# A later wait for the group-mean matrix, row loads issued one per key store, and unread products on TensorE around the attention

## The chip, the cores and the metric

One core of a Trainium2 chip runs the whole program in one launch. The metric is the device time of one execution in microseconds. The core has TensorE (PE, with its weight loads shown as PEld), VectorE (DVE), ScalarE (ACT), GpSimd (POOL) and SyncE (SP), which run side by side and wait for each other on semaphores. SyncE, ScalarE and GpSimd each issue DMA transfers on a queue of their own (q1, q10 and q0 in the profile), and 16 DMA engines serve all queues.

## The reference

The input x is four images of 128 channels and 96 x 96 pixels. Two layers follow each other:

```
x = x + L0(_gn(x))        # group norm over 32 groups of 4 channels, then attention over channels
x = x + L1(_gn(x))        # group norm, then sign, 3x3 conv, batch norm, sign, 3x3 conv, batch norm, + identity

L0: kv = dw3x3(einsum(qkv_w, x));  k, v = split(kv)
    q  = idwt2(dw3x3 of the four bands of dwt2(x))       # wavelet transform, convs, inverse transform
    q, k normalised along the pixels;  attn = softmax(q k^T * temperature) in each of 8 heads of 16 channels
    out = proj_w @ (attn @ v)
L1: out = conv3x3(sign(x), sign(w1)*alpha1);  out = sign(batchnorm(out))
    out = batchnorm(conv3x3(out, sign(w2)*alpha2)) + x
```

## The kernel before

The program has four blocks. Each is a set of five instruction streams, one for each engine, and a block begins when all streams of the one before it have ended.

**Block 1, `block_stats_and_projections`** (lines 187 to 530). For every image it takes the statistics for the group norm and multiplies the image with the key and value weights. An image has 24 chunks of 4 rows (384 pixels); 4 chunks are a piece, so there are 6 pieces an image and 24 in all, counted n = 0 to 23. For each piece TensorE makes 4 key chunks and 4 value chunks, ScalarE copies them out of PSUM (line 477), VectorE makes the low half of the keys (line 429), and two stores of 784 KB leave: the keys from SyncE's queue (line 288), the values from ScalarE's queue (line 481). Both go through a ring of three buffers: before ScalarE writes the first key chunk of piece n it waits until the key store of piece n - 3 has landed. After the store of piece 6, SyncE also issues seven constants for block 2 (lines 296 to 298), and then eight loads of x rows (`load_x_rows`, line 175), each 144 KB in runs of 384 bytes, for the first two channel groups. The store of piece 7 comes behind them in SyncE's stream. These loads write into the memory of image 0, which is why they wait until image 0 is used up.

**Block 2, `block_grams`**. It makes queries, keys and their gram matrices, channel group by channel group. It is bound by TensorE for 670 us and is not changed, but for products added behind its last instruction on TensorE, `gram_null` (line 1121).

**Block 3, `block_attention`** (lines 1201 to 1376). It works on matrices of 16 x 16 numbers. TensorE and VectorE take turns: products `rows` (lines 1358, 1359) and 32 small ones (1365); VectorE lines 1285 to 1304; product `pn` (1369); VectorE and ScalarE to line 1320; product `pq` (1372); `abd` (1331); four products (1375); the copy of `pa_t` (1337) ends the block. Meanwhile SyncE loads the weights of the convolutions, and then image 0 of x and of the values in halves (lines 1258, 1259, 2304 KB each, signals `s_v0` and `s_x0`).

**Block 4, `block_convolutions`** (lines 1379 to 1770). For each image, TensorE projects the values (`project`, line 1749), VectorE adds x (`add_x`, line 1631) and takes statistics (1635), `group_mean` multiplies them with the matrix `gmean` (1738), ScalarE takes the signs (1537), and TensorE convolves (1761) while it projects the next image. x lives in `xs`, which has room for two images. GpSimd loads images 1 to 3 into it (`load_x`, line 1503) and stores the finished sums of images 0 and 1 (line 1513), each in four parts, and waits for each part to land before it issues the next: load of image 1, store of image 0, load of image 2, store of image 1, load of image 3. VectorE waits for all four parts of image b + 1 before its first `add_x` of that image.

The matrix `gmean` (64 KB) is loaded by SyncE at the start of block 4 with signal `s_c`. TensorE and VectorE both wait for `s_c` before their first instruction of the block, though only `group_mean` reads the matrix, and it first runs after the 24 projections of image 0.

Of the kernel before, what the change touches and what calls it, by code (L numbers as in the profile page):

```python
# [22 lines left out]
F32 = mybir.dt.float32  # L23
F16 = mybir.dt.float16
# [160 lines left out]
def block_stats_and_projections(nc, d, p):  # L185

    with ExitStack() as ctx:
# [83 lines left out]
        def _(sp):  # L271
# [13 lines left out]
            for n in range(NIMG * NPC):  # L285
# [4 lines left out]
                if n == NPC:  # L290
# [7 lines left out]
                    sp.dma_start(early["null_cols"], d["null_cols"].partition_broadcast(W)).then_inc(p["s_c"], 16)  # L298
                    for i in range(2):
                        for im in range(NIMG):  # L300
                            load_x_rows(sp, d, early, im, i, i, p["s_xin"][i])
                if n == (NIMG - 1) * NPC:
# [227 lines left out]
def block_grams(nc, d, p):  # L530
# [5 lines left out]
    with ExitStack() as ctx:  # L536
# [518 lines left out]
        def _(pe):  # L1055
# [140 lines left out]
            for e in range(GPARTS - 1):  # L1196
                gram_part(HEADS - 1, (HEADS - 1) % 2, e, 0, len(units[e]), last_banks[e], e > 0)
            gram_null(HEADS - 1, last_banks[GPARTS - 1], True)


def block_attention(nc, d, p):

    with ExitStack() as ctx:
# [28 lines left out]
        pn = ctx.enter_context(nc.psum_tensor("b3_pn", [C, 512], F32))  # L1232
        pp = ctx.enter_context(nc.psum_tensor("b3_pp", [C, 512], F32))

        s_in, s_g, s_gst = p["s_in"], p["s_g"], p["s_gst"]
# [114 lines left out]
        def _(pe):  # L1350
            pe.wait_ge(s_in, NSMALL * 16)
            pe.wait_ge(s_g, 32)
            pe.wait_ge(s_gst, GRAMS_IN)

            def rows(bank, sel, one, two, last, stop=True):

# [7 lines left out]
            for n in range(HI):  # L1364
                ins = nc.tensor.matmul(ps[0:HD, n * HD:(n + 1) * HD], gram[:, n, 2, :], pick[:, HD:2 * HD],
                                       start=False, stop=(n == HI - 1))
            ins.then_inc(s_p, 1)
            pe.wait_ge(s_go, 1)
            nc.tensor.matmul(pn[0:HD, 0:HI * HD], ones[:], krow[:].rearrange("p n e -> p (n e)"),
                             start=True, stop=True).then_inc(s_p, 1)  # L1370
            pe.wait_ge(s_go, 2)
            nc.tensor.matmul(pq[:, 0:HI * HD], copies[:], att[:].rearrange("p n e -> p (n e)"), start=True, stop=True).then_inc(s_p, 1)
# [6 lines left out]
def block_convolutions(nc, d, p):  # L1379
# [5 lines left out]
    with ExitStack() as ctx:  # L1385
# [222 lines left out]
        def _(dve):  # L1608
# [66 lines left out]
            dve.sem_inc(s_y, NBK)  # L1675
            dve.wait_ge(s_c, 16)
            for half in range(2):
# [54 lines left out]
        def _(pe):  # L1732
            pe.wait_ge(s_c, 16)

            def group_mean(b):
# [31 lines left out]
            for half in range(2):  # L1767
                pe.wait_ge(p["s_v0"][half], 16)
                with pe.Fori(half * RND // 2, (half + 1) * RND // 2) as r:
                    for k in range(RC):  # L1770
                        project(0, r, k)
            group_mean(0)
            for b in range(NIMG - 1):
# [110 lines left out]
```

## Time and profile before

| | |
|---|---|
| median of 3 runs | 1374.42 us (1373.09 to 1375.93) |
| profiled execution | 1371.92 us, of which the span of instructions 1370.0 us |
| PE busy | 1182.8 us (86%) |
| DVE busy | 1025.6 us (75%) |
| ACT busy | 889.5 us (65%) |
| POOL busy | 433.7 us (32%) |
| blocks, from the timeline | block 1: 0 to 187 us; block 2: to 879; block 3: to 906; block 4: to 1370 |

A timeline row gives the start, the duration, the engine, the line, the operation and its tiles, the count of instructions merged in it, and in brackets how long the engine was idle before it and what released it. `SPq` and `POOLq` are the sequencers. The table of windows gives for each stretch the busy time and count of instructions of every engine, then the granted clock of TensorE (1.00 is 2.4 GHz, 0.50 is 1.2 GHz), the share of the 16 DMA engines' time that was in use, and GB/s.

### The profile page before, as it was taken

Reading aid. Unit: us, or ns where it says so; the run is one execution under the profiler, and the core shown is the slowest. Engines: PE = TensorE matmul, PEld = TensorE weight load, DVE = VectorE, ACT = ScalarE, POOL = GpSimd, SP = SyncE. Lnnn points to the kernel's source line nnn. Section 1 sums busy time; section 2 is a strip of 40 time slices with the busy share of each in tenths; the row PEclk is TensorE's granted clock in tenths of the full one; section 3 lists DMA queues with packets and bytes.
Section 4 is the critical chain, followed back from the end, with each engine's and each line's share of the span. In section 5 each row is a group of like instructions: output and inputs, shape, how many; then the busy total and the mean of one; then the engine's idle time right before and its main releaser. Section 6 shows DMA issues by size and latency. Waiting matters only on the chain. (4 is left out here: it accounts for less than half of the span.)

```text
span 1370.0 us, 33894 instructions
## 1 busy us (share of the span) xinstructions
PE 1182.8 (86%) x12758; PEld 929.9 (68%) x12758; DVE 1025.6 (75%) x1771; ACT 889.5 (65%) x1574; POOL 433.7 (32%) x476
## 2 busy tenths in 40 slices
PE   0997989999999999999999999748999997999900
PEld 0553658999999999999999999414555554555500
DVE  6776547999999999999999999258666643163494
ACT  0666887888888889888889886013244255766382
POOL 6200034555565655656556554100000010000010
PEclk9999988999999999999999999869999999999955
DMA  9997872544544535534534532386775230000079
GB/s 331 418 268 284 298 266 75 138 102 129 135 109 130 149 94 134 146 94 134 147 101 126 150 104 74 126 350 223 261 257 184 77 121 0 1 0 0 0 309 398
DMA packets 146919, 220.71 MB, mean 161 GB/s; under 512 B 115000, under 2 KB 116196, under 8 KB 142176
## 3 DMA queue, kind: packets, MB, share of 16 engines
q1 hardware_dynamic: 135696, 151.97, 36.9%
q0 software_dynamic: 6480, 47.19, 9.0%
q10 hardware_dynamic: 4608, 19.67, 3.6%
q8 instruction: 95, 1.56, 0.5%
q14 instruction: 40, 0.33, 0.1%
HBM read 131.58 MB, written 86.93 MB: 159 GB/s over the span
## 5 line engine op out<-in xcount | busy, mean ns | idle before, releaser
L1761 PE MATMUL b_conv_bank<-b_sign,wsign 128*128 (+1 forms) x1728 | 297.6, 329 | 10.3 <-ACT b_sign L1537 7.7
L1761 PEld LDWEIGHTS b_conv_bank<-b_sign,wsign 128*128 128x128 bf16 x1728 | 168.9, 98 | 142.2 <-issue 29.9
L824 POOL TENSOR_TENSOR b_vacc<-b_vacc 128x576 f32<-128x576 f32 x128 | 180.4, 1410 | 195.0 <-ACT b_vacc L919 194.2
L1060 PE MATMUL b_bank<-b_tkh,x_first 96*96 96x100 f16 x1536 | 220.9, 210 | 2.4 <-DVE b_tml L1041 2.4
L1062 PE MATMUL b_bank<-b_tkh,x_first 96*96 96x100 f16 x1536 | 220.7, 210 | 0.0
L1061 PE MATMUL b_bank<-b_tkl,x_first 96*96 96x100 f16 x1536 | 220.6, 210 | 0.0
L1060 PE MATMUL b_bank<-x_first,b_tmh 96*96 96x200 f16 x768 | 195.1, 254 | 15.0 <-DVE b_yl L1025 10.0
L1018 DVE SCALAR_TENSOR_TENSOR b_value_sum<-b_vin,value_taps,b_value_sum 128x576 f32<-128x576 f32 x256 | 206.6, 807 | 0.0
L1060 PEld LDWEIGHTS b_bank<-b_tkh,x_first 96*96 96x96 f16 x1536 | 193.2, 126 | 4.0 <-DVE b_tml L1041 2.7
L1062 PE MATMUL b_bank<-x_first,b_tml 96*96 96x200 f16 x768 | 193.6, 252 | 0.0
L1062 PEld LDWEIGHTS b_bank<-b_tkh,x_first 96*96 96x96 f16 x1536 | 193.2, 126 | 0.0
L1061 PE MATMUL b_bank<-b_yl,b_tmh 96*96 96x200 f16 x768 | 192.2, 250 | 0.0
L1061 PEld LDWEIGHTS b_bank<-b_tkl,x_first 96*96 96x96 f16 x1536 | 191.7, 125 | 0.0
L965 ACT CAST b_feat<-b_bank 96x400 f16<-96x400 f32 x255 | 124.5, 488 | 86.7 <-PE b_bank L1062 86.1
L919 ACT ACTIVATE b_vacc<-b_vin,value_taps 128x576 f32<-128x576 f32 x192 | 149.4, 779 | 24.8 <-POOL b_vacc L824 12.5
L753 POOL TENSOR_TENSOR b_xl<-x_first,b_xh 96x384 f16<-96x384 f32 x128 | 130.4, 1040 | 83.3 <-ACT b_xh L913 83.3
L1025 DVE TENSOR_TENSOR b_feat<-b_bank,b_feat 96x400 f16<-96x400 f32 x256 | 144.1, 563 | 11.8 <-ACT b_feat L965 8.9
L1060 PEld LDWEIGHTS b_bank<-x_first,b_tmh 96*96 96x96 f16 x768 | 94.3, 123 | 27.6 <-DVE b_yl L1025 16.9
L1025 DVE TENSOR_TENSOR b_tml<-b_bank,b_tmh 96x504 f16<-96x504 f32 (+1 forms) x155 | 99.4, 641 | 16.8 <-ACT b_tmh L965 16.8
L1642 DVE BATCH_NORM_STATS2 b_bny<-x_first (+1 forms) x96 | 53.4, 558 | 74.4 <-ACT x_first L1556 74.2
L526 PE MATMUL b_pk<-b_x,b_w_image 128*128 128x384 f32 x288 | 99.4, 500 | 11.2 <-DVE b_khl L429 11.2
L1556 ACT CAST x_first<-b_conv_bank 128x384 f32 (+1 forms) x96 | 45.7, 479 | 92.1 <-PE b_conv_bank L1761 91.3
(230 smaller groups left out, 2688.2 us busy)
## 6 DMA issues: line engine op xcount, KB each, us to landing
b_vin<-value_projection_scratch SPq DMA_DIRECT2D x32, 686.0 KB, 5.8
keys_scratch<-b_khl SPq DMA_DIRECT2D x24, 784.0 KB, 4.7
value_projection_scratch<-b_vout ACTq DMA_DIRECT2D x24, 784.0 KB, 5.4
x_first<-keys_scratch SPq DMA_DIRECT2D x128, 147.0 KB, 3.0
x_first<-in_x SPq DMA_DIRECT2D x128, 144.0 KB, 5.3
values_scratch<-b_vacc SPq DMA_DIRECT2D x32, 576.0 KB, 3.4
out<-xs SPq DMA_DIRECT2D x25, 576.0 KB, 6.7
b_x<-in_x POOLq DMA_DIRECT2D x9, 1536.0 KB, 19.8
```

The costliest lines, as they stand in the source:

```text
L526: nc.tensor.matmul(psum_k[g % NBK][:, 0:CH], w_image[:, b % 2, v, :], image(b)[:, at:at + CH], start=True, stop=True).then_inc(s_mm, 1)
L753: nc.gpsimd.tensor_tensor(xh[1][:, slot, im, :, :].rearrange("h c w -> h (c w)"), xraw[:, slot, im * GC * W:(im + 1) * GC * W], xh[0][:, s ...
L824: nc.gpsimd.tensor_tensor(whole, whole, room, ALU.add).then_inc(s_padd, 1)
L919: return nc.scalar.activation(out.rearrange("p (r c) -> p r c", c=W), src, ACT.Copy, scale=vtaps[:, t:t + 1])
L965: nc.scalar.copy(*target(n, 0, k)).then_inc(s_hi, 1)
L1018: nc.vector.scalar_tensor_tensor(whole if t == 8 else part, src, vtaps[:, t:t + 1], whole if t == 3 else part, ALU.mult, ALU.add).then_inc ...
L1025: nc.vector.tensor_tensor(out, src, high, ALU.subtract).then_inc(s_dve, 1)
L1060: nc.tensor.matmul(out, w_hi, m_hi, start=first, stop=False)
L1061: nc.tensor.matmul(out, w_hi, m_lo, start=False, stop=False)
L1062: return nc.tensor.matmul(out, w_lo, m_hi, start=False, stop=last)
L1642: V.bn_stats(bny[:, ds(r * RC + (b * NCH + k), 1), :].rearrange("p o s -> p (o s)"), y_of(b)[:, ds(r * (RC * CH) + k * CH, CH)]).then_inc( ...
L1761: ins = nc.tensor.matmul(cbank[k % NBK][:, 0:CH].rearrange("p (r c) -> p r c", c=W), p["wsign"][nth // NIMG][:, t * C:(t + 1) * C], padded ...
```

## The change

In block 1 the eight loads of x rows no longer follow the constants in one go. One is issued behind each of the key stores of pieces 7 to 14. At the end of block 2, TensorE gets 34 products of 256 columns whose result nobody reads. In block 3 it gets 24 such products after the product that ends at line 1365 and 34 after `pn`; they go to a PSUM bank of their own and take `copies`, a tile of 16 partitions, as both operands. In block 4 VectorE no longer waits for `s_c`, and TensorE waits for it ahead of the first `group_mean` instead of ahead of the first projection.

```diff
@@ block_stats_and_projections, sync @@
-                    for i in range(2):
-                        for im in range(NIMG):
-                            load_x_rows(sp, d, early, im, i, i, p["s_xin"][i])
+                if NPC < n <= NPC + 2 * NIMG:
+                    i, im = divmod(n - NPC - 1, NIMG)
+                    load_x_rows(sp, d, early, im, i, i, p["s_xin"][i])
@@ block_grams, tensor @@
             gram_null(HEADS - 1, last_banks[GPARTS - 1], True)
+            for _ in range(34):
+                nc.tensor.matmul(bank[4][:, 0:4 * HD * RUN], map_place[:, 0:2 * HD * RUN], map_place[:, 0:4 * HD * RUN],
+                                 start=True, stop=True)
@@ block_attention @@
+        unused = ctx.enter_context(nc.psum_tensor("b3_unused", [C, 512], F32))
@@ block_attention, tensor @@
+            def keep_busy(many):
+                tile = copies[:].bitcast(F16)
+                for _ in range(many):
+                    nc.tensor.matmul(unused[:, 0:4 * HD * RUN], tile[:, 0:2 * HD * RUN], tile[:, 0:4 * HD * RUN],
+                                     start=True, stop=True)
             ins.then_inc(s_p, 1)
+            keep_busy(24)
             pe.wait_ge(s_go, 1)
             nc.tensor.matmul(pn[0:HD, 0:HI * HD], ones[:], krow[:].rearrange("p n e -> p (n e)"),
                              start=True, stop=True).then_inc(s_p, 1)
+            keep_busy(34)
             pe.wait_ge(s_go, 2)
@@ block_convolutions, vector @@
-            dve.wait_ge(s_c, 16)
@@ block_convolutions, tensor @@
-            pe.wait_ge(s_c, 16)
                     for k in range(RC):
                         project(0, r, k)
+            pe.wait_ge(s_c, 16)
             group_mean(0)
```

## Rows read from the trace of the kernel before

**Rows 1.** Waits of the span: engine, line, releaser; us, times, longest
```profile
ACT b_khl L477 <- DMA keys_scratch<-b_khl: 8.4, 2, 7.9
PE b_proj_bank L1749 <- DMA b_gmean<-in_group_mean: 10.7, 1, 10.7
```

**Rows 2.** Timeline of ACT in block 1, first key chunk of pieces 7 and 15
```profile
81.08 0.59 ACT L477 ACTIVATE b_khl<-b_pk,b_bias 128x384 f16<-128x384 f32 x1 [1.05 <-PE b_pk L526]
...
139.63 2.13 ACT L477 ACTIVATE b_khl<-b_pk,b_bias 128x384 f16<-128x384 f32 x4 [0.46 <-PE b_pk L526]
```

**Rows 3.** Windows: pieces 9 and 11 of image 1, 15 and 17 of image 2
```profile
95.12:107.96 12.84, 8.17 (x27) 4.59 (x25) 2.83 (x8) 4.45 (x8) 0.00 (x0) 0.97 1.10 370
...
113.56:119.86 6.30, 6.30 (x22) 3.77 (x22) 3.69 (x12) 4.68 (x9) 0.00 (x0) 0.97 0.49 192
139.63:145.01 5.38, 5.38 (x19) 3.26 (x18) 2.83 (x8) 4.45 (x8) 0.00 (x0) 1.00 0.83 340
...
150.17:155.80 5.63, 5.63 (x21) 3.48 (x20) 3.69 (x12) 4.45 (x8) 0.00 (x0) 1.00 0.49 196
```

**Rows 4.** Timeline of SP: the eight loads of x rows
```profile
86.71 12.29 SPq L175 DMA_DIRECT2D x_first<-in_x  x8
```

**Rows 5.** DMA packets in the windows 92:94, 95:97 and 657.5:662.5 us
```profile
DMA packets 33, 0.05 MB, mean 24 GB/s; under 512 B 9, under 2 KB 31, under 8 KB 33
...
DMA packets 805, 0.77 MB, mean 384 GB/s; under 512 B 711, under 2 KB 711, under 8 KB 805
...
DMA packets 1051, 1.54 MB, mean 308 GB/s; under 512 B 803, under 2 KB 803, under 8 KB 1051
```

**Rows 6.** Timeline of block 3: the four turns of PE, and PE's last products before
```profile
868.50 5.62 PE L1108 MATMUL b_bank<-b_feat 96*128 96x256 f16 x50
...
879.83 1.86 PE L1358 MATMUL b_pq<-x_first 128*16 128x512 f32 x2 [4.81 <-DMA x_first<-x_first]
...
886.88 1.02 PE L1359 MATMUL b_ps<-x_first 128*16 128x512 f32 x2
...
893.58 1.88 PE L1369 MATMUL b_pn<-b_krow,b_ones 16*16 16x512 f32 x2 [4.09 <-DVEq L1305]
900.29 2.07 PE L1372 MATMUL b_pq<-b_att,x_first 16*128 16x512 f32 x2 [4.83 <-DVEq L1321]
```

**Rows 7.** Timeline of DVE in block 3: its start after PE's first turn
```profile
886.28 0.68 DVE L1285 TENSOR_TENSOR b_diag<-b_pq,x_first 16x512 f32<-16x512 f32 x1 [5.64 <-PE b_pk L1359]
```

**Rows 8.** Window in which the granted clock rises in block 3
```profile
884.00:886.00 2.00, 2.00 (x4) 0.39 (x3) 0.00 (x0) 0.00 (x0) 0.00 (x0) 0.65 1.01 406
```

**Rows 9.** Timeline: issue of gmean, first projection, first sums of images 1 and 3
```profile
906.42 0.33 SPq L1474 DMA_DIRECT2D b_gmean<-in_group_mean  x1
...
916.02 8.45 PE L1749 MATMUL b_proj_bank<-y_first,pa_t 128*128 x18 [10.67 <-DMA b_gmean<-in_group_mean]
...
943.24 0.56 DVE L1631 TENSOR_TENSOR xs<-b_proj_bank,xs 128x384 f32<-128x384 f32 x1
...
1055.23 0.54 DVE L1631 TENSOR_TENSOR xs<-b_proj_bank,xs 128x384 f32<-128x384 f32 x1
```

**Rows 10.** x of image 0: first issue; median of two; most of xs, 860:930
```profile
884.09 0.45 SPq L1259 DMA_DIRECT2D xs<-in_x  x1
...
xs<-in_x SPq DMA_DIRECT2D x2, 2304.0 KB, 22.7
...
DMA to landing us min/median/max: 5.4/8.7/27.9
```

**Rows 11.** Timeline of POOL: fourth parts of images 1, 3; below, tile xs, 930:1060
```profile
930.40 0.53 POOL L1503 DMA_DIRECT2D xs<-in_x  x1 [5.99 <-issue]
...
1042.93 0.53 POOL L1503 DMA_DIRECT2D xs<-in_x  x1 [6.95 <-issue]
...
DMA to landing us min/median/max: 4.4/6.0/8.0
```

**Rows 12.** DMA queues in the window 907 to 910.5 us
```profile
q1 hardware_dynamic: 193, 1.37, 93.4%
```

## The prediction

> **What bounds the kernel now.** I read the list of waits first, to see which waits the change addresses, and it shows both: ScalarE once waits 7.9 us for a key store, and TensorE 10.7 us for the group-mean matrix [rows 1]. Then I read the timeline around each, to see whether anything else was late at the same moment, and last the windows, for the granted clock and the DMA traffic. The kernel has no single bound. Block 1 is a pipeline of ScalarE, TensorE and VectorE fed by a ring of three buffers; block 2 is TensorE alone; block 3 is a chain of short turns between TensorE and VectorE; block 4 begins with a DMA wait, and is TensorE from then on, with GpSimd's loads of the images close behind. So each edit is read in its own place, and a gain in blocks 1 or 3 moves all that follows, unless a load does not move with it.
>
> **Part 1, row loads one per key store.** SyncE spends 12.29 us, from 86.71 us on, to issue eight row loads [rows 4]; the store of piece 7 is issued only then, at 99.0, lands at about 107.9, and piece 10 needs its buffer. Piece 9 therefore lasts 12.84 us, and the clock is lost in the pause. Pieces 9 to 11 run from 95.12 to 119.86, 24.74 us; the same pieces of the next image, 15 to 17, run from 139.63 to 155.80, 16.17 us [rows 3]. The difference, 8.6 us, is all there is to win. After the change store 7 is issued some 12 us earlier, and has to be home by 100.0, when ScalarE now begins to wait.
>
> Something still stands in front of it: the seven constants. Between 92 and 94 us the 16 DMA engines moved 24 GB/s in 33 packets, of which only 9 were under 512 bytes, as the row loads' packets are; between 95 and 97 us 711 such small packets went through, and the rate was 384 GB/s [rows 5]. So the slow transfers are the constants with their longer packets, and they are over at about 95 us wherever the row loads stand. Behind them wait the key and the value store of piece 7, 1.61 MB together, or 4.2 us at 384 GB/s: they land at about 99.2, just before 100.0. I take 0.4 us for the part that may still stick out: part 1 gives 8.2 us. Its bounds are 8.6 (nothing sticks out) and about 4 (store 7 lands 4 us late). Of the eight loads each also costs traffic. Four of them had block 2's window to themselves, 1.54 MB with other transfers at 308 GB/s [rows 5]; one load of 147 kB is then 0.5 us of DMA, beside 4.2 us for the two stores of a piece, under the 5.2 us of the quickest piece. That hides them. ScalarE's own value stores are not behind them in a queue, and no other queue is passed. Block 2 wants the rows at 187 us; the last load goes out behind store 14, near 130.
>
> A rule of the Trainium skill speaks against this part (DMA: Bandwidth & Descriptors, Specifications): transfers under 512 bytes miss the full rate, since each becomes a read and a write of its target. The trace agrees in direction, 308 against 384 GB/s, and in nothing that would change the sum.
>
> **Part 2, unread products.** In block 3 TensorE starts its first turn at 1.2 GHz: two passes of 512 columns take 1.86 us there and 1.02 us once the clock is up [rows 6], which happens within 884 to 886 us [rows 8]. VectorE starts at 886.28 [rows 7], 6.45 us after TensorE. Eight passes at 2.4 GHz, 0.43 us each (two back to back are 0.86 and the last drains for 0.16), are 3.4, and with the same 0.7 us of handing over VectorE would start at 883.9: 2.3 us. The clock falls again in the pause, and the third and fourth turns take 1.88 and 2.07 us [rows 6]; at 2.4 GHz they give 0.8 and 0.55 us, the fourth cut short because VectorE is in the reduction of line 1325 until 901.9. The last products may give another 0.5. Sum 3.7 to 4.2 us if the clock holds. The cost: 50 products of 256 columns took 5.62 us [rows 6], 0.112 each. The 34 at the end of block 2 run from 875.0 to 878.8, hidden by SyncE's last stores (block 3 starts at 879.3). The 24 end near 889.4, VectorE asks for `pn` at 891.2. The 34 after `pn` end near 896 and `pq` is asked for at 897. Queued behind them is only that next product. If products on 16 partitions do not hold the clock, which no row shows, the last 34 take 7.6 us and `pq` comes up to 3 us late: part 2 is then 2.3 less 3, about -1. Bounds -1 to 4.2; I take 4, since the two holes left are under 2 us.
>
> **Part 3, the later wait.** The matrix is issued at 906.42 and TensorE starts at 916.02 [rows 9]. Without it TensorE would start at about 906.6, if the first halves are in. The two halves of x are issued at 884.1 and a microsecond later, and take 22.7 us in the median of two and 27.9 at most [rows 10], so the first took 17.5 and was in at 901.6, the second at 913; the values go ahead of each. So 9.4 us go here, and with part 2 the path of TensorE and VectorE is 13.4 us earlier. VectorE comes to the wait for the second half only at about 914 (a start at 902, then half of the 25 us that it took for image 0). The wait for `s_c` before `group_mean` costs nothing: the matrix is 10 us old.
>
> **What is late next** decides these two parts. GpSimd's chain of loads and stores does not start earlier through part 3 at all. Its last part of image 1 is issued at 930.40 and lands in some 6.0 us, the median of its transfers; with 0.2 for handing over that is 936.6. VectorE's first sum of image 1 was at 943.24 [rows 9, 11], so that sum gains at most 6.6 us, not 13.4. The chain goes on waiting for nothing but its own transfers. The last part of image 3 is issued at 1042.93, so it is there at 1049.1, and the first sum that needs it was at 1055.23 [rows 9, 11]: 6.1 us are left; image 2 lies between the two. After that only TensorE counts. If the start of block 4 moves by part 2, does the chain move? Between 907 and 910.5 us, with GpSimd's first load issued at 907.40, all data packets but one were SyncE's (193, none on q0) [rows 12]: it stood behind the halves of image 0, whose end part 2 does not move. So I keep the chain where it is, and take **6.1 us for parts 2 and 3 together**. With that part 2 is worth nothing of its own at the end: 9.4 alone is already above the bound.
>
> **The sum.** 8.2 + 6.1 = 14.3 us. The profiled execution of before has 1371.92 us (span 1370.0 and 1.9 around it), 2.5 below the median 1374.42. I expect a profiled execution near 1357.6 and a median of 1360.1.
>
> **Rivals.**
> - *The image loads move with block 4.* A load of GpSimd takes turns with SyncE's backlog instead of standing behind it, so that the chain starts with the block, up to 4.2 us earlier by part 2. For: every later load began within a microsecond or so. Against: [rows 12]. It gives 8.2 + 6.1 + 4.2 = 18.5, or 1355.9 us. The Trainium skill says this (DMA: Bandwidth & Descriptors, Queues, rings and completion order): each DMA engine goes round its queues packet by packet. By that rule this rival would be the forecast; the trace of this window does not agree. Chance 0.17.
> - *Store 7 stays late.* The constants and the two stores need until 104 instead of 99; ScalarE still waits 4 us. 4.2 + 6.1 = 10.3, or 1364.1 us. For: the margin is under 1 us, and the constants' end is seen only in total traffic. Chance 0.15.
> - *The matrix was not the last thing.* If the first half of x is really what ends near 913, block 4 hardly moves: 8.2 + 2 = 10.2, or 1364.2 us. Against: [rows 10]. Chance 0.05.
> - *The row loads were the slow transfers* (the slower side). If a load of 147 kB moves at the 24 GB/s of 92 to 94 us it takes 6.1 us; with 4.2 for the stores a piece takes 10.3, and eight take 82 us. Pieces 7 to 14 took 58.6 (81.08 to 139.63 [rows 2]), 50 without the stall. That is 32 lost against 8.6 + 6.1 won: 17 us slower, 1391 us. It decides from 4.3 us a load on: 8 x (4.2 + 4.3) = 68, less 50, is more than 14.7 by 3. Against: [rows 5]. Chance 0.04.
>
> **How the numbers follow.** Forecast 0.55, with its own range 1357.5 to 1362.5 (the chain a microsecond either way, since stores now meet other value loads, and part 1 by 0.4 to 1); rivals 0.17, 0.15, 0.05, 0.04; 0.04 for less than expected everywhere. The range 1354 to 1366 takes in all but the slow rival and the last. About 0.2% (2.7 us) is what a measurement of this kernel can tell from no change. Faster 0.93, same 0.03, slower 0.04.
>
> **What the profile after would show.** Part 1: ScalarE's wait for a key store is gone or under 1 us, row loads stand between key stores, block 2 begins near 179. Part 2: clock 1.00 through block 3, VectorE's first start 4.6 us after TensorE's instead of 6.45, block 3 of 23 us instead of 27. Part 3: the first projection within 0.5 us of the block's start; a new wait of VectorE for `xs` loads before image 1 (some 6 us) and a short one before images 2 or 3. The prediction is wrong if that new wait is missing, if the first GpSimd load begins at once, or if piece 10 still waits.

## The result, and the profile after

The changed kernel has a median of 1357.51 us (1354.76 to 1359.28), the kernel before in the same runs 1373.76 us (1372.54 to 1375.93). The ratio is 0.9885, with a 95% interval of 0.9863 to 0.9908. Measured again later, the changed kernel took 1354.02 us (1351.64 to 1354.75) beside 1369.2 us, ratio 0.9892 (0.9866 to 0.9919). The forecast was 1360.1 us, with a range of 1354 to 1366. A ratio here comes with its result, formed over runs taken side by side; it can differ by 0.2% from the quotient of the medians beside it. The kernel before was some 4 us slower in the first measurement than in all later ones, so medians from different groups of runs compare only through their ratios.

I cut each profiled execution at three instructions of SyncE's timeline, the first load of block 2, the first load of block 3 and the load of `gmean`:

| us | before | after | after, again |
|---|---|---|---|
| profiled execution | 1371.92 | 1358.03 | 1354.08 |
| span | 1370.0 | 1356.1 | 1352.2 |
| block 1 | 187.6 | 179.6 | 180.0 |
| block 2 | 691.7 | 689.0 | 691.2 |
| block 3 | 27.1 | 26.5 | 26.5 |
| block 4 | 463.6 | 461.0 | 454.5 |
| first projection after the start of block 4 | 9.60 | 0.38 | 0.38 |

**Part 1.** This is ScalarE's timeline of the changed kernel, key chunks of pieces 9 to 12. It answers to [rows 3].

```profile
95.70 2.13 ACT L477 ACTIVATE b_khl<-b_pk,b_bias 128x384 f16<-128x384 f32 x4 [0.46 <-PE b_pk L526]
101.79 2.00 ACT L477 ACTIVATE b_khl<-b_pk,b_bias 128x384 f16<-128x384 f32 x4 [1.16 <-DMA keys_scratch<-b_khl]
106.25 2.13 ACT L477 ACTIVATE b_khl<-b_pk,b_bias 128x384 f16<-128x384 f32 x4 [0.46 <-PE b_pk L526]
111.88 2.11 ACT L477 ACTIVATE b_khl<-b_pk,b_bias 128x384 f16<-128x384 f32 x4 [0.48 <-PE b_pk L526]
```

The 7.9 us for a key store [rows 1] have become 1.16 us. Pieces 9 to 11 now last 111.88 - 95.70 = 16.18 us, where they lasted 24.74 [rows 3]. SyncE's timeline shows why; it answers to [rows 4], and a store is now always followed by one row load:

```profile
89.18 0.34 SPq L288 DMA_DIRECT2D keys_scratch<-b_khl  x1
89.57 0.72 SPq L175 DMA_DIRECT2D x_first<-in_x  x1
94.58 0.34 SPq L288 DMA_DIRECT2D keys_scratch<-b_khl  x1
94.97 0.65 SPq L175 DMA_DIRECT2D x_first<-in_x  x1
```

**Part 2.** TensorE's timeline around block 3 answers to [rows 6]:

```profile
864.28 3.89 PE L1200 MATMUL b_bank<-x_first 126*128 126x256 f16 x34
869.13 1.02 PE L1369 MATMUL b_pq<-x_first 128*16 128x512 f32 x2 [0.96 <-DMA x_first<-x_first]
...
875.96 2.79 PE L1363 MATMUL b_unused<-x_first 16*128 16x256 f16 x24
880.12 1.88 PE L1381 MATMUL b_pn<-b_krow,b_ones 16*16 16x512 f32 x2 [1.36 <-DVEq L1309]
881.93 7.43 PE L1363 MATMUL b_unused<-x_first 16*128 16x256 f16 x34
889.16 1.91 PE L1385 MATMUL b_pq<-b_att,x_first 16*128 16x512 f32 x2
```

The pair of passes that took 1.86 us takes 1.02: the first turn is now at 2.4 GHz. But the product `pn` still takes 1.88 us, and the 34 unread products behind it 7.43 us or 0.22 each, twice the 0.112 of [rows 6]. The windows of the same stretch say that the clock had fallen to 1.2 GHz (columns as in [rows 8]; the last three are clock, DMA share, GB/s):

```profile
874.00:878.00 4.00, 4.00 (x85) 3.40 (x83) 3.42 (x8) 1.51 (x2) 0.00 (x0) 1.00 0.70 257
878.00:880.00 2.00, 0.75 (x7) 0.41 (x5) 1.83 (x6) 0.03 (x1) 0.00 (x0) 0.76 1.00 424
880.00:884.00 4.00, 3.88 (x12) 1.53 (x13) 2.68 (x6) 0.00 (x0) 0.00 (x0) 0.50 1.02 438
```

VectorE's timeline shows what each half is worth. It starts at 872.82, 3.7 us after TensorE instead of 6.45 [rows 7]; and later it waits for `pq`, which stood behind the 34 products:

```profile
872.82 0.68 DVE L1289 TENSOR_TENSOR b_diag<-b_pq,x_first 16x512 f32<-16x512 f32 x1 [2.85 <-PE b_pk L1370]
...
891.18 0.69 DVE L1335 TENSOR_TENSOR b_abd<-b_pq,x_first 128x512 f32<-128x512 f32 x1 [2.77 <-PE b_pq L1385]
```

**Part 3.** TensorE begins block 4 at once (its timeline), and VectorE waits for images instead (its timeline, images 1 and 2). Both answer to [rows 9]; line 1759 was 1749, and 1644 was 1631:

```profile
895.51 8.70 PE L1759 MATMUL b_proj_bank<-y_first,pa_t 128*128 x18 [1.45 <-DVEq L1687]
```

```profile
925.07 0.56 DVE L1644 TENSOR_TENSOR xs<-b_proj_bank,xs 128x384 f32<-128x384 f32 x1 [1.86 <-DMA xs<-in_x]
985.84 0.56 DVE L1644 TENSOR_TENSOR xs<-b_proj_bank,xs 128x384 f32<-128x384 f32 x1 [6.01 <-DMA xs<-in_x]
```

The second wait is the difference between the two profiles of the same kernel. The repetition has only the first, of 1.69 us, and its block 4 is 6.5 us shorter. I had expected both waits again, of 4 to 9 us in all, and a block 4 of 460 to 465 us; the repetition missed that. TensorE feels the wait for image 2 behind VectorE, and then runs at 1.2 GHz for a while (timeline, then the window, columns as above):

```profile
986.45 4.21 PE L1759 MATMUL b_proj_bank<-b_values,pa_t 128*128 128x384 f32 x6 [8.71 <-DVE xs L1644]
```

```profile
984.00:988.00 4.00, 1.55 (x3) 0.90 (x4) 2.09 (x5) 0.00 (x0) 0.54 (x1) 0.50 0.02 9
```

### The profile page after: what moved, and what is told of

Its sections match the earlier page's. It is cut to its first block and busy times, and to the rows that moved or that the text cites. A ratio compares the mean times of both kernels' runs of the same rounds, so it can differ in the third digit from the quotient of the medians.

```text
span 1356.1 us, 34077 instructions
## 1 busy us (share of the span) xinstructions
PE 1187.9 (88%) x12850; PEld 935.9 (69%) x12850; DVE 1026.2 (76%) x1771; ACT 889.0 (66%) x1574; POOL 433.0 (32%) x476
## 5 line engine op out<-in xcount | busy, mean ns | idle before, releaser
L1025 DVE TENSOR_TENSOR b_feat<-b_bank,b_feat 96x400 f16<-96x400 f32 x256 | 143.6, 561 | 8.5 <-ACT b_feat L965 6.4
L1025 DVE TENSOR_TENSOR b_tml<-b_bank,b_tmh 96x504 f16<-96x504 f32 (+1 forms) x155 | 99.2, 640 | 16.7 <-ACT b_tmh L965 16.7
L1569 ACT CAST y_first<-b_conv_bank 128x384 f16<-128x384 f32 (+1 forms) x96 | 45.6, 476 | 89.1 <-PE b_conv_bank L1771 87.8
```

What stands on the lines that cost most here:

```text
L1025: nc.vector.tensor_tensor(out, src, high, ALU.subtract).then_inc(s_dve, 1)
L1569: nc.scalar.copy(dst, cbank[k % NBK][:, 0:CH]).then_inc(s_y, 1)
```

## Experiments

Each kernel was profiled and timed. The table has their blocks, with the time at which VectorE adds the first rows of images 1, 2 and 3, counted from the start of block 4 (its timeline, the first sum of the form `128x384 f32<-128x384 f32` of each image). Where VectorE waits for a load of GpSimd, they show how late the load is; the text takes the groups one by one.

| kernel | median us | block 1 | 2 | 3 | 4 | image 1, 2, 3 |
|---|---|---|---|---|---|---|
| before | 1373.76 | 187.6 | 691.7 | 27.1 | 463.6 | 36.8, 92.6, 148.8 |
| row loads alone | 1362.32 | 181.1 | 689.1 | 27.2 | 463.2 | 37.6, 93.3, 149.2 |
| later wait alone | 1363.04 | 187.9 | 687.4 | 27.3 | 453.2 | 30.2, 84.9, 140.1 |
| products alone | 1368.85 | 187.8 | 691.4 | 26.5 | 464.4 | 37.7, 93.5, 148.1 |
| after | 1357.51 | 179.6 | 689.0 | 26.5 | 461.0 | 29.9, 90.7, 147.1 |
| after, again | 1354.02 | 180.0 | 691.2 | 26.5 | 454.5 | 29.8, 84.7, 140.6 |
| after without products | 1355.04 | 178.5 | 688.9 | 25.9 | 462.1 | 30.5, 89.1, 146.5 |
| products on 128 partitions | 1353.78 | 179.5 | 687.3 | 22.8 | 464.8 | 33.4, 93.2, 150.1 |
| constants later | 1353.68 | 180.3 | 689.0 | 26.5 | 457.8 | 29.6, 84.6, 143.7 |
| image 1 early | 1352.68 | 179.9 | 689.0 | 26.5 | 454.7 | 27.7, 83.5, 139.7 |
| image 1 early, no products | 1352.54 | 181.1 | 690.9 | 26.1 | 455.2 | 29.0, 85.0, 141.1 |
| no waits for parts | 1350.17 | 178.6 | 689.2 | 26.5 | 453.9 | 27.6, 83.5, 139.5 |
| no waits, 128 partitions | 1347.64 | 178.6 | 688.9 | 22.3 | 455.1 | 29.0, 87.1, 141.8 |
| no waits, first 16 of that tile | 1353.87 | 181.7 | 691.0 | 26.5 | 454.4 | 28.8, 85.6, 141.6 |

The kernel before had medians of 1369.7, 1369.96, 1369.2 and 1370.35 us beside these groups.

### Each part by itself

The row loads alone, the kernel before with

```diff
-                    for i in range(2):
-                        for im in range(NIMG):
-                            load_x_rows(sp, d, early, im, i, i, p["s_xin"][i])
+                if NPC < n <= NPC + 2 * NIMG:
+                    i, im = divmod(n - NPC - 1, NIMG)
+                    load_x_rows(sp, d, early, im, i, i, p["s_xin"][i])
```

> The kernel before with the row loads spread over the key stores, and nothing else. Theory: the stall of piece 10 goes and nothing takes its place, block 1 ends 8.0 to 8.6 us earlier, and since block 2 is TensorE alone all of it stays: 8 us faster, ratio 0.994. Rival (the slow constants still hold store 7 back in most executions, the changed kernel was lucky): a wait of 3 to 4 us of ScalarE for a key store, 4 to 5 us faster.

Measured: 1362.32 us (1355.91 to 1363.16), ratio 0.9926 (0.9897 to 0.9954). Block 1 ends at 181.1; piece 10 waits 1.73 us. No other block moves by more than its own spread. That is 7.4 us between the medians, near the 8 expected and above the 4 to 5 of the rival.

The later wait alone, the kernel before with

```diff
-            dve.wait_ge(s_c, 16)
...
-            pe.wait_ge(s_c, 16)
...
                         project(0, r, k)
+            pe.wait_ge(s_c, 16)
             group_mean(0)
```

> The kernel before with the later wait for the group-mean matrix, and nothing else. Theory (GpSimd's chain of loads and stores takes the place of the wait): the first projection starts 9.2 us earlier, VectorE then waits some 5 to 6 us for x of image 1 and again for image 2 or 3, and the end is 2 to 4 us earlier. Rival (the chain stretched in the changed kernel only because the unread products moved block 4 against the backlog of loads): 6 us earlier here. Rival (no bound behind the wait): 9 us.

Measured: 1363.04 us (1357.12 to 1364.61), ratio 0.9942 (0.9917 to 0.9966). Its timed runs lie in two heaps, at 1357 and at 1363 to 1365, and the profiled execution, 1357.64, is of the lower one; there VectorE waits only once for an image, 1.65 us, and block 4 is 10.4 us shorter. Block 2 is 4.3 us shorter too, which an edit behind it can't cause. The edit gains 6.7 us between the medians, more than the 2 to 4 that my theory gave, though a wait for an image does take the place of the old one; 6 us had been the rival's number, and the two heaps leave room for either.

The products alone, the kernel before with the three groups of unread products of the change.

> The kernel before with the unread products, and nothing else. Theory (products whose operands lie on 16 partitions do not hold the clock): block 3 is 26.3 us instead of 27.0, the first turn gains 2.7, the last 34 products run at 1.2 GHz for 7.4 us and delay the next turn by 2.4. The end is 0 to 1 us earlier, no difference to be measured. Rival (the products at the end of block 2 keep more than block 3 at the high clock): 3 us faster.

Measured: 1368.85 us (1366.33 to 1374.41), ratio 0.9993 (0.9978 to 1.0009).

The other way round, the changed kernel without them:

```diff
-            for _ in range(34):
-                nc.tensor.matmul(bank[4][:, 0:4 * HD * RUN], ...)
...
-            keep_busy(24)
...
-            keep_busy(34)
```

> The changed kernel without its unread products (parts 1 and 3 remain). Theory: within 1 us of the changed kernel, 1357 to 1359 us, block 3 27 us long again. If the products carried the 2.7 us by which block 2 became shorter in the profile of the changed kernel: block 2 is 691.8 us long again and the time is 1360 to 1361.

Measured: 1355.04 us (1349.15 to 1357.23), ratio 0.9872 (0.9847 to 0.9898); the changed kernel had 0.9885 and 0.9892. Parts 1 and 3 are the whole change; the ratios of the three parts multiply to 0.986. Block 3 is 25.9 us here and not the 27 expected, shorter than with the products. By both tests the products are worth nothing that can be measured.

### What keeps the clock up in block 3

The changed kernel, with the same number of products of the same columns, on a tile of 128 partitions:

```diff
-                tile = copies[:].bitcast(F16)
+                tile = pick[:].bitcast(F16)
                 for _ in range(many):
-                    nc.tensor.matmul(unused[:, 0:4 * HD * RUN], tile[:, 0:2 * HD * RUN], tile[:, 0:4 * HD * RUN],
-                                     start=True, stop=True)
+                    nc.tensor.matmul(unused[:, 0:4 * HD * RUN].rearrange("p (a b) -> p a b", a=2), tile,
+                                     tile.unsqueeze(1).broadcast_to([2 * HD * RUN, 2, 2 * HD * RUN]), start=True, stop=True)
```

> The changed kernel, with the unread products of the attention block reading a tile of 128 partitions instead of `copies` with its 16; count and columns stay (24 and 34 of 256 columns). Theory A (few partitions do not keep the clock up): with 128 partitions the granted clock is 1.00 through block 3, the 34 products take some 3.8 us instead of 7.43, the product `pq` is no longer late, and block 3 is 23 to 24.5 us instead of 26.5. Theory B (the clock falls in the pauses whatever the products read): block 3 stays at 26 to 27 us and the products at 7.4. The end: if GpSimd's chain of loads moves with block 4, the median goes down by the same 2 to 3 us against the changed kernel (ratio to before 0.986 to 0.987); if the loads stay behind SyncE's transfers, by under 1 us (0.988).

Measured: 1353.78 us (1352.08 to 1356.34), ratio 0.988 (0.9843 to 0.9916). Block 3 is 22.8 us. TensorE's timeline and windows:

```profile
874.12 2.79 PE L1363 MATMUL b_unused<-x_first 128*128 128x256 f16 x24
878.28 1.03 PE L1381 MATMUL b_pn<-b_krow,b_ones 16*16 16x512 f32 x2 [1.37 <-DVEq L1309]
879.24 5.55 PE L1363 MATMUL b_unused<-x_first 128*128 128x256 f16 x34
884.72 1.12 PE L1385 MATMUL b_pq<-b_att,x_first 16*128 16x512 f32 x2
```

```profile
880.00:884.00 4.00, 4.00 (x24) 2.87 (x23) 3.11 (x6) 2.39 (x3) 0.00 (x0) 0.57 0.98 419
884.00:888.00 4.00, 3.08 (x17) 2.00 (x15) 3.43 (x5) 0.34 (x1) 0.00 (x0) 0.90 1.00 424
```

The clock holds through `pn`, falls for a few us after it, and is back before `pq`. So theory A was right about block 3, which became even a little shorter than the 23 to 24.5 us expected, and too hopeful about "1.00 throughout". The end didn't gain: against the first profile of the changed kernel block 3 is 3.7 us shorter and block 4 3.8 us longer.

The two tiles also differ in content and access pattern. Another kernel takes the first 16 partitions of the same tile, in the kernel that is described under GpSimd's chain:

```diff
-                tile = pick[:].bitcast(F16)
+                tile = pick[0:HD, :].bitcast(F16)
...
-                                     tile.unsqueeze(1).broadcast_to([2 * HD * RUN, 2, 2 * HD * RUN]), start=True, stop=True)
+                                     tile.unsqueeze(1).broadcast_to([HD, 2, 2 * HD * RUN]), start=True, stop=True)
```

> The kernel with both edits (GpSimd not waiting for each part, unread products on the 128 partitions of `pick`), but its unread products take only the first 16 partitions of the same tile; tile, access pattern, columns and count are the same. If it is the number of partitions that decides whether the products keep the clock up, block 3 is 26.3 to 26.6 us again, the 34 products take 7.4 us at a granted clock of 0.50, and the time is 2 to 4 us more. If it was something else about the other tile (its contents, or the form of its access pattern), block 3 stays near 22.5 us and the 34 products at 3.8 to 5.6 us.

Measured: 1353.87 us (1350.01 to 1355.53), ratio 0.9877 (0.9853 to 0.99). TensorE's timeline with 16 partitions, then with 128:

```profile
880.03 2.79 PE L1363 MATMUL b_unused<-x_first 16*128 16x256 f16 x24
884.18 1.88 PE L1381 MATMUL b_pn<-b_krow,b_ones 16*16 16x512 f32 x2 [1.37 <-DVEq L1309]
886.00 7.43 PE L1363 MATMUL b_unused<-x_first 16*128 16x256 f16 x34
893.23 1.91 PE L1385 MATMUL b_pq<-b_att,x_first 16*128 16x512 f32 x2
```

```profile
874.89 2.79 PE L1363 MATMUL b_unused<-x_first 128*128 128x256 f16 x24
879.04 1.03 PE L1381 MATMUL b_pn<-b_krow,b_ones 16*16 16x512 f32 x2 [1.36 <-DVEq L1309]
880.00 3.89 PE L1363 MATMUL b_unused<-x_first 128*128 128x256 f16 x34
884.91 1.12 PE L1385 MATMUL b_pq<-b_att,x_first 16*128 16x512 f32 x2 [1.02 <-DVEq L1325]
```

The 24 products take 2.79 us in both, the pause behind them is the same 1.4 us, and only the number of partitions differs. With 16 the clock is down when `pn` starts (1.88 us), with 128 it is up (1.03). The granted clock is 0.50 from 884 to 890 us with 16, and 1.00 from 878 to 888 with 128. Block 3 is 26.5 against 22.3 us. That shows the cause. The other profiles agree: `pn` took 1.88 or 1.89 us in all seven with products on 16 partitions, and 1.03 in both with 128. By the ratios, 0.9877 against 0.9861, the time is 2.2 us more, as expected; between the medians it is 6.2, since blocks 1 and 2, which this edit doesn't touch, came out 5.2 us longer.

### GpSimd's chain of loads

Does it bind block 4, and does it hang on the block's start? GpSimd's timeline, first the changed kernel, then the one with products on 128 partitions:

```profile
896.09 0.62 POOL L1516 DMA_DIRECT2D xs<-in_x  x1
906.41 0.53 POOL L1516 DMA_DIRECT2D xs<-in_x  x1 [9.69 <-issue]
913.00 0.53 POOL L1516 DMA_DIRECT2D xs<-in_x  x1 [6.07 <-issue]
```

```profile
890.53 0.62 POOL L1516 DMA_DIRECT2D xs<-in_x  x1
903.77 0.53 POOL L1516 DMA_DIRECT2D xs<-in_x  x1 [12.61 <-issue]
910.64 0.53 POOL L1516 DMA_DIRECT2D xs<-in_x  x1 [6.35 <-issue]
```

Counted from the start of block 3 (868.6 and 866.8 us), the first part is issued at 27.5 and 23.8 us, but the second at 37.8 and 37.0. It was at 37.9 in the kernel before, and at 37.5 to 38.4 in the other six profiles with the chain as it is. So in the second kernel the first part is issued 3.7 us earlier and is home only 0.8 us earlier. The DMA queues of that kernel, 890 to 894 us and then 894 to 898 (packets, MB, time):

```profile
q1 hardware_dynamic: 111, 1.77, 104.2%
...
q1 hardware_dynamic: 61, 1.11, 64.7%
q0 software_dynamic: 59, 0.54, 32.4%
```

In the time without packets the load doesn't wait for SyncE's transfers to end. Read in steps of 0.2 us, q0's first packet comes 3.4 to 3.8 us after the issue in all twelve profiles that begin with this load, whether it is issued 23.3 or 28.2 us after the start of block 3, and 3.8 us after it in the two kernels below whose first transfer is a store at 35 us. Behind the eleven transfers that follow, in three of the profiles, it is 1.0 to 2.6 us. What makes the first one slow no run here shows. From then on the queues take turns, 59 packets against 61. But a packet of SyncE's halves is twice as long, 18 KB against 9, so q0 moves 0.54 of 1.65 MB. At that rate the 1.18 MB of the first part need 8.7 us, and with the 3.6 us in front 12.3; it landed 12.1 us after its issue. In the changed kernel it meets short packets of SyncE, moves 0.28 to 0.34 MB in a microsecond and lands after 9.2 us. The start moves with the block; the landing hardly does.

The next kernel takes image 1 out of the chain; SyncE loads it behind image 0:

```diff
+            for k in range(2):
+                half = slice(k * (HW // 2), (k + 1) * (HW // 2))
+                sp.dma_start(p["xs"][:, 1, half], d["x_c"][:, 1, half]).then_inc(p["s_x1"], 16)
...
-            load_x(1)
...
-                dve.wait_ge(s_x[b], RND * 16)
+                dve.wait_ge(s_x[b] if b else p["s_x1"], RND * 16 if b else 32)
...
+        p["s_x1"] = ctx.enter_context(nc.semaphore("second_image_in"))
```

> The changed kernel, with image 1 of x loaded by SyncE in two halves behind those of image 0, in the attention block, and left out of GpSimd's chain. If the chain of GpSimd's loads is what took back part of the 9.4 us of the removed wait, VectorE waits for no image any more, block 4 is 452 to 455 us instead of 461 and the time some 7 us less than that of the changed kernel: ratio 0.983 to 0.985. If block 4 is bound by TensorE alone from image 1 on, nothing moves: 0.988 to 0.989. If the new load delays the matrix, which now stands behind 4.7 MB more on SyncE's queue, the first group-mean product waits for it: some 33 us after the block's start are needed for the projections, and 12 us more of transfers in front of it would put the matrix at 22 us, so I expect no wait there.

Measured: 1352.68 us (1351.73 to 1354.68), ratio 0.988 (0.9843 to 0.9917). Block 4 is 454.7 us, no image is waited for, and `group_mean` doesn't wait for the matrix, as expected. The time is not 7 us under the changed kernel's: by the ratios it is 0.7 to 1.6 us (0.988 against 0.9885 and 0.9892), which can't be told from nothing. I had counted from the worse of its two profiles.

The same without any unread products:

> As the kernel before last in this call (image 1 of x loaded early by SyncE), and without any of the unread products. If the products are worth nothing at the end, the time is within 1 us of that kernel. If they hold the clock of TensorE for the beginning of block 4 or shorten block 3 by the 0.6 us seen in one profile, it is 0.5 to 3 us longer.

Measured: 1352.54 us (1348.81 to 1355.16), ratio 0.9866 (0.9825 to 0.9906), so again no difference.

The next kernel leaves the order of the chain, and takes out the wait for each part (a store still waits for its sums, and the next load of the same memory for the four parts of the store):

```diff
                     pool.dma_start(xs[:, b % 2, piece], d["x_c"][:, b, piece]).then_inc(s_x[b - 1], 16)
-                    pool.wait_ge(s_x[b - 1], r * 16 + 16)
-                    pool.sem_inc(s_carry, 1)
...
                     pool.dma_start(d["x1"][:, b, piece], xs[:, b, piece]).then_inc(s_xst, 16)
-                    pool.wait_ge(s_xst, r * 16 + (b * RND * 16 + 16))
-                    pool.sem_inc(s_carry, 1)
+                pool.wait_ge(s_xst, (b + 1) * RND * 16)
```

> The changed kernel, with GpSimd in block 4 no longer waiting for each part of a load or store to land before it issues the next; it waits once for the four parts of a store. If the chain's length is made of round trips, image 1 is in well before VectorE asks for it, VectorE's waits of 1.9 and 6.0 us for x go, and block 4 is 452 to 455 us: ratio 0.983 to 0.985. If the parts then only crowd the DMA engines (the four together take as long as four in turn, 26 us and more) the waits stay and block 4 is 460 to 463 us: 0.988 to 0.990.

Measured: 1350.17 us (1350.08 to 1350.30), ratio 0.9858 (0.9822 to 0.9893). GpSimd's timeline:

```profile
895.28 0.62 POOL L1516 DMA_DIRECT2D xs<-in_x  x1
896.27 0.53 POOL L1516 DMA_DIRECT2D xs<-in_x  x1 [0.37 <-issue]
897.22 0.53 POOL L1516 DMA_DIRECT2D xs<-in_x  x1 [0.42 <-issue]
898.17 0.53 POOL L1516 DMA_DIRECT2D xs<-in_x  x1 [0.43 <-issue]
902.84 0.54 POOL L1524 DMA_DIRECT2D x_scratch<-xs  x1 [4.14 <-DVE xs L1641]
```

Four loads are under way at once, the first store goes out at 902.84, where the changed kernel's goes out at 926.19, and from 895 to 922 us the queues move 419 GB/s. All waits for images are gone. The chain was long because of its round trips, not its bytes. By the ratio the kernel is 3.7 to 4.7 us faster than the changed one, though the intervals overlap, and the 0.983 to 0.985 expected was just missed. The four timed runs lie within 0.22 us; that may be chance, since the two other kernels without these waits spread over 4.6 and 5.5 us.

With both edits together:

> The changed kernel with both edits of earlier runs: GpSimd does not wait for each part in block 4, and the unread products of the attention read 128 partitions. With the chain in place the shorter block 3 was worth nothing at the end (block 4 was 3.8 us longer). If it was the chain that ate it, it counts now: block 3 near 22.8 us, block 4 near 454 us, the profiled span near 1345 us, the time 3 to 4 us less than without the second edit and some 8 to 10 us less than the changed kernel. If something else binds block 4 to the clock on the wall (SyncE's halves of image 0), block 4 grows to 457 us and the time stays within 1 us of the kernel without the second edit.

Measured: 1347.64 us (1346.85 to 1351.40), ratio 0.9861 (0.9837 to 0.9885), against 1354.02 us of the changed kernel beside it: 6.4 us less, where I expected 8 to 10. Block 3 is 22.3 us and block 4 455.1. Freed of the chain, block 4 is 9.7 us shorter than behind the same products with the chain (464.8), so in the profile the short block 3 reaches the end: against the kernel with the first edit alone it is 4.2 us shorter, and block 4 only 1.2 us longer. That it is faster than the kernel with the first edit alone isn't shown by the times: the medians are 2.5 us apart, from different groups of runs, and the ratios are equal (0.9861 and 0.9858). The profiled executions are 3.2 us apart.

### The constants in front of store 7

The prediction held the seven constants, not the row loads, for the slow transfers [rows 5]. Here they are issued behind the key store of piece 15:

```diff
-                    for name in ("ana", "map_place", "key_place", "map_diag", "key_diag"):
...
+                if n == NPC + 2 * NIMG + 1:
+                    for name in ("ana", "map_place", "key_place", "map_diag", "key_diag"):
```

> The changed kernel, with the seven constants for block 2 issued behind the key store of piece 15 instead of that of piece 6. If they were the slow transfers in front of the key store of piece 7, piece 10 no longer waits (1.16 us in the changed kernel's profile, 0.5 to 1.7 in others), no window near 90 us moves under 100 GB/s, the slow window turns up near 145 us instead, and block 1 is 0.5 to 1 us shorter. If the row loads were the slow ones, the wait of piece 10 stays at 0.5 to 1.7 us. Where the constants delay another key store, one of pieces 17 to 19 waits for up to 5 us and block 1 is as much longer.

Measured: 1353.68 us (1351.12 to 1356.39), ratio 0.989 (0.986 to 0.9919). Store 7 lands 7.2 us after its issue instead of 12.6 (the list of DMA issues), at 97.1, where it landed at 98.6 to 103.9 in the ten profiles with the edit of part 1 and the constants in their old place. Piece 10 doesn't wait, but neither does it in three of those ten. And block 1 gains nothing, where I had expected 0.5 to 1 us: from SyncE's store of piece 7 to its end it takes 180.33 - 89.94 = 90.39 us, and 179.62 - 89.18 = 90.44 in the changed kernel. Nor does the slow stretch move along. Windows of this kernel where the constants now run:

```profile
136.00:138.00 2.00, 2.00 (x7) 1.17 (x7) 0.04 (x1) 1.44 (x3) 0.00 (x0) 1.00 0.97 398
...
140.00:142.00 2.00, 2.00 (x8) 1.18 (x7) 0.60 (x2) 1.87 (x4) 0.00 (x0) 1.00 0.92 250
```

and, a microsecond each, where the stores of piece 7 run without them:

```profile
90.00:91.00 1.00, 1.00 (x4) 0.60 (x5) 1.00 (x3) 0.14 (x1) 0.00 (x0) 1.00 3.22 320
91.00:92.00 1.00, 1.00 (x5) 0.60 (x4) 1.00 (x3) 0.94 (x2) 0.00 (x0) 1.00 0.57 19
92.00:93.00 1.00, 1.00 (x5) 0.52 (x3) 0.96 (x3) 0.83 (x3) 0.00 (x0) 1.00 0.45 25
93.00:94.00 1.00, 0.86 (x5) 0.46 (x4) 0.85 (x2) 1.00 (x2) 0.00 (x0) 1.00 0.00 0
94.00:95.00 1.00, 1.00 (x4) 0.60 (x4) 1.00 (x3) 0.30 (x2) 0.00 (x0) 1.00 0.88 364
```

The value store, issued at 88.50, starts at full rate. Then next to nothing moves from 91 to 94 us, and the key store, issued at 89.94, has its first packets only after 94. So the constants are not slow in themselves; they moved at 250 to 400 GB/s with the stores around them. In all fourteen profiles the stretch from 91 to 94 us moves only 15 to 133 GB/s, with the constants or without. VectorE is busy in nearly all of it, but just as busy from 90 to 91 and from 94 to 95, where the rate is 320 and 364; what else holds the transfers up stays open.

## Why the prediction was right, point by point

**Part 1: 8.2 us predicted.** From ScalarE's first key chunk of piece 7 to the end of block 1 it was 187.6 - 81.08 = 106.5 us, and is 179.62 - 81.66 = 97.96; so 8.6 us, the upper bound. The same stretch is 106.5 to 107.1 us in the three profiles without the edit, 97.9 to 98.0 in eight of the eleven with it, and 98.5 to 98.8 in the other three. The term that was off is the 0.4 us "that may stick out". Store 7 landed at about 101.8, not at 99.2, and ScalarE waited 1.16 us, over the "under 1 us" that I had named, so the sign of being wrong, that piece 10 still waits, did come. Yet that wait costs nothing, since pieces 9 to 11 take the same 16.18 us with it as pieces 15 to 17 [rows 3] without it; the three profiles with waits of 1.7 to 2.1 us lose 0.5 to 0.9. The rival in which store 7 stays late had the direction of the landing right and the price wrong. That the slow transfers are the constants, and that the rate is back once they are over, was a wrong reading of [rows 5]: from 91 to 94 us the transfers are as slow without them. The rival in which the row loads are slow is out: eight loads between the stores, and no piece grew.

**Part 2: 4 us if the clock holds, worth nothing at the end.** The step that failed is the first one: products on 16 partitions don't hold the clock. I had looked at the length of the holes and not at the partitions. The 34 at the end of block 2, on 126 partitions, do hold it; they give the first turn 2.75 us (6.45 to 3.7; I had 2.3). The 24 and 34 on 16 partitions give nothing, and the 34 delay `pq`: from `pn` to `pq` it is 9.04 us (880.12 to 889.16), and was 6.71 [rows 6], so 2.3 late, where I had "up to 3". Together 2.75 - 2.33 = 0.4, in the lower part of the bounds and not the 4 that I took, and block 3 is 0.6 us shorter in this pair of profiles. Even that is not all the products' doing: with them block 3 is 26.5 us in all seven profiles on 16 partitions, and without any it is 27.1, 27.2, 27.3, 25.9 and 26.1 us. In the two short ones the first turn came to 2.4 GHz in its second or third pair of passes, in the others in the fourth. With products on 128 partitions it was 22.3 to 22.8 us, as forecast. The second step, that this is worth nothing at the end, held in the hardest case: with the clock kept up block 4 gave the 3.7 us back.

**Part 3, and what is late next: 6.1 us for parts 2 and 3.** The first projection follows the block's start by 0.38 us, so the whole wait went, 9.2 us. With the chain as it is, block 4 was 461.0, 454.5, 453.2, 462.1 and 457.8 us (leaving out the kernel on 128 partitions), in the mean 457.7; without the edit 463.6, 463.2 and 464.4, in the mean 463.7. Blocks 3 and 4 together, with that kernel taken in, have 480.5 to 488.0 us, in the mean 484.8, against 490.7 without the edit: 5.9 us. Kernels with the chain out of the way have 453.9 to 455.2 for block 4: 9 us, the whole of the wait. So the sum held as a mean over six profiles, and that the chain takes the wait's place held too: the first sum of image 1 comes 7.5 us earlier counted from the start of block 3 (63.9 to 56.4; I had 6.6), where VectorE now waits for its load. For a single execution it was luck: the six gain 2.7 to 10.2 us. The waits were mis-sized: I had 6 us before image 1, from a part 2 worth 4; it was 1.9, and 5.3 in the kernel where block 3 really was short. And which image binds changes from execution to execution. I had image 3 (148.8 less 6.1 is 142.7); it was 147.1, 140.6, 140.1, 146.5 and 143.7, in the mean 143.6. A part takes 6 to 9 us, twenty follow one another, and I had given their sum a microsecond either way. It is four to five.

**The rival that the image loads move with block 4** had the mechanism right and the price wrong, and with it a step of the forecast fails: GpSimd's first load did not stand behind the halves of image 0. [rows 12] end 3.1 us after its issue, when it has no packet in any profile. In the kernel whose block 3 is 3.7 us shorter its packets came 3.9 us earlier against the start of block 3 and took turns with SyncE's. The Trainium skill's rule for it (DMA: Bandwidth & Descriptors, Queues, rings and completion order), that every DMA engine goes round its queues packet by packet, agrees with the trace: 59 packets against 61 from 894 to 898 us. But with SyncE's packets twice as long the load took 12.1 us instead of 9.2, and the second part came only 0.8 us earlier, not the 4.2 of the rival. So "I keep the chain where it is" came out right for a reason that the trace doesn't bear out.

**The rest.** The matrix was the last thing waited for, so that rival is out. Block 2 was 2.7 us shorter in the first profile, and nobody had forecast it; in the repetition it is 691.2. Over all fourteen profiles it is 687.3 to 691.7, in the kernels without part 1 as in those with it (mean 690.2 and 689.4), so that is spread, not effect. It made the first profile look better than the working: its span fell by 8.0 us in block 1, 2.7 in block 2 and 3.2 in blocks 3 and 4, 13.9 in all, so block 2 by luck gave most of what blocks 3 and 4 lacked of their 6.1. Taken part by part over the profiles, 8.6 + 5.9 = 14.5 us, against 14.3 forecast and 16.3 and 15.2 between medians. That the trace agrees in direction with the Trainium skill's rule on short transfers was a wrong reading of [rows 5]: the faster window, at 384 GB/s, has the larger share of packets under 512 bytes (711 of 805 against 803 of 1051 at 308). The range of 1354 to 1366 held, by less on its fast side than I thought: the repeated measurement lies at its edge.

## What to carry to other kernels

When a wait is moved off the path, ask which chain does not move with it: how late its last part is, not the removed wait, sets the gain. A chain of transfers, each waited for before the next is issued, adds up its round trips and their scatter; where order alone is needed, issue them together and wait once. Before putting a queue's silence down to another queue's backlog, look how long its first packet takes after the issue elsewhere. Work that is meant to keep TensorE's clock up should be of the shape that is seen to do so in the same trace, and a filler in front of a product on the path costs double if it fails.

## What the runs showed of the hardware that I had not expected

- Unread products with operands on 16 partitions didn't keep the clock at 2.4 GHz and the same products on 128 partitions did: `pn` took 1.88 and 1.03 us, the 34 products 7.43 and 3.89. A kernel with 128 partitions could still lose it for a few us (5.55).
- The same constants were on their way when the DMA engines moved 24 GB/s, between 92 and 94 us ([rows 5]), and moved at 250 to 400 GB/s between 136 and 142. Without them, the stores were as slow there: 19, 25 and 0 GB/s in the three microseconds from 91 us. The cause is open.
- The first packet of GpSimd's first transfer came 3.4 to 3.8 us after its issue in all fourteen profiles, beside a busy q1, and 1.0 to 2.6 us after it for the eleven transfers behind it in three of them. Two queues that took turns packet by packet did not share the bytes evenly: 0.54 of 1.65 MB with packets of 9 and 18 KB.
- Block 2, which no edit touches before its last instruction, took 687.3 to 691.7 us from one profile to another, and the last of the twenty transfers was issued 139.5 and 130.8 us after the start of block 4 in two profiles of the changed kernel.
